# Six stages of a two-layer attention kernel under one block, with a hand-drawn SBUF map and PSUM rings per use

## The reference

```python
# layer 0: cross attention, both sides with an adaptive norm
xq  = (1 + scale_q) * ln(x)   + shift_q        # scale, shift = silu(cond) @ Wss_q + bss_q
xkv = (1 + scale_k) * ln(ctx) + shift_k
x1  = x + softmax(q @ k.T / sqrt(32)) @ v @ Wp + bp
# layer 1
c   = silu(cond) @ W_mod + b_mod               # six vectors of width 512 per batch
qkv = modulate(ln(x1), shift_a, scale_a) @ W_qkv + b_qkv
x2  = x1 + gate_a * (attention(q, k, v) @ W_proj + b_proj)
x3  = x2 + cross_attention(ln(x2) @ W_qc, ln(ctx) @ W_kvc) @ W_cproj + b_cproj
out = x3 + gate_m * (gelu(modulate(ln(x3), shift_m, scale_m) @ W1 + b1) @ W2 + b2)
```

## Time and profile before

| | |
|---|---|
| median of three runs | 2728.22 us |
| profiled execution | 2728.28 us |
| its span (first to last instruction) | 2726.5 us |
| PE busy | 2485.6 us (91%) |
| DVE, ACT, POOL busy | 1393.7 (51%), 1121.4 (41%), 584.0 us (21%) |
| mean granted TensorE clock | 0.94 |

### The profile page before, as it was taken

One profiled execution on the slowest core, in us unless ns is written; L12 is line 12 of the kernel. 1 busy time (PEld: TensorE's weight loads), 2 busy tenths in 40 slices (PEclk: granted clock), 3 DMA queues, 4 the chain that ended last, 5 costly groups with the idle time before them and its releaser, 6 DMA issues. The chain is left out here.

```text
span 2726.5 us, 33092 instructions
## 1 busy us (share of the span) xinstructions
PE 2485.6 (91%) x12304; PEld 1738.5 (64%) x12304; DVE 1393.7 (51%) x2467; ACT 1121.4 (41%) x2007; POOL 584.0 (21%) x321
## 2 busy tenths in 40 slices
PE   5789999879997899999998789999889999999998
PEld 5666666568885344444443366666568888888887
DVE  4346766644444776767676456766534222222221
ACT  5335554334442445555554344444334322332231
POOL 1101111100000356666664501211110000000000
PEclk9878999889998799999998878999889999999999
DMA  7565766545545555544553276767443011101110
GB/s 246 157 189 154 211 189 165 146 153 185 181 178 167 119 123 134 141 122 109 135 125 98 67 195 175 202 180 189 134 129 96 1 54 55 54 1 55 55 39 16
DMA packets 229647, 349.17 MB, mean 128 GB/s; under 512 B 41636, under 2 KB 73468, under 8 KB 229487
## 3 DMA queue, kind: packets, MB, share of 16 engines
q1 hardware_dynamic: 228318, 343.21, 44.2%
q0 software_dynamic: 1168, 3.85, 0.4%
HBM read 228.73 MB, written 116.69 MB: 127 GB/s over the span
## 5 line engine op out<-in xcount | busy, mean ns | idle before, releaser
L1438 DVE TENSOR_REDUCE self_negated_max<-banks 128x1 f32<-128x512 f32 x512 | 334.2, 678 | 161.5 <-PE banks L1505 159.9
L1595 ACT ACTIVATE self_exponentials<-banks 128x512 f32<-128x512 f32 x512 | 287.8, 594 | 305.2 <-PE banks L1526 147.5
L1411 POOL TENSOR_TENSOR self_exponentials<-self_exponentials 128x2048 f32<-128x2048 f32 x64 | 299.7, 4682 | 248.0 <-ACT self_exponentials L1595 248.0
L1956 PE MATMUL banks<-mlp_w_mlp_hi,mlp_hidden_parts 128*128 128x512 f32 x1024 | 334.9, 389 | 1.5 <-DVE mlp_hidden_parts L1914 1.5
L1914 DVE TENSOR_TENSOR mlp_hidden_parts<-mlp_wide,mlp_hidden_parts 128x512 fp32r<-128x512 f32 x128 | 92.9, 726 | 396.9 <-ACT mlp_hidden_parts L1979 396.9
L293 POOL TENSOR_SCALAR norm_rstd<-norm_mean_var 128x4 f32<-128x4 f32 x32 | 8.4, 264 | 1311.4 <-DVE norm_mean_var L265 1311.3
L1505 PE MATMUL banks<-self_key_stack,self_query_stack 96*128 96x512 f32 x512 | 227.6, 456 | 43.4 <-DVE self_negated_max L1438 24.7
L1974 ACT ACTIVATE mlp_wide<-banks,bias_columns 128x512 f32<-128x512 f32 x128 | 88.3, 690 | 425.7 <-PE banks L357 425.7
L1526 PE MATMUL banks<-self_query_stack,self_key_stack 98*128 98x512 f32 x512 | 231.9, 458 | 13.8 <-DVE self_negated_max L1438 9.3
L1956 PEld LDWEIGHTS banks<-mlp_w_mlp_hi,mlp_hidden_parts 128*128 128x128 f32 x1024 | 192.2, 188 | 41.9 <-DVE mlp_hidden_parts L1914 2.0
L1526 PEld LDWEIGHTS banks<-self_query_stack,self_key_stack 98*128 98x128 f32 x512 | 97.9, 192 | 183.3 <-ACT self_exponentials L1595 101.0
(11 more groups left out here) (219 smaller groups left out, 5134.2 us busy)
## 6 DMA issues: line engine op xcount, KB each, us to landing
L_query_stack<-q_parts_L SPq DMA_DIRECT2D x96, 256.0 KB, 4.4
norm_x<-x SPq DMA_DIRECT2D x24, 1024.0 KB, 7.2
self_query_stack<-q_parts_self SPq DMA_DIRECT2D x96, 256.0 KB, 4.1
self_key_stack<-k_parts_self SPq DMA_DIRECT2D x96, 256.0 KB, 6.5
cross_query_stack<-q_parts_cross SPq DMA_DIRECT2D x96, 256.0 KB, 4.5
q_parts_L<-L_query_parts SPq DMA_DIRECT2D x32, 512.0 KB, 4.6
q_parts_self<-qkv_qk_parts SPq DMA_DIRECT2D x32, 512.0 KB, 3.5
k_parts_self<-qkv_qk_parts SPq DMA_DIRECT2D x32, 512.0 KB, 2.8
```

The lines of the kernel that those rows point to most:

```text
L1411: e.tensor_tensor(self.p[kt - 1][:], self.p[kt - 1][:], self.p[kt][:], ALU.add).then_inc(self.paired.sem, 1)
L1438: e.tensor_reduce(self.nm[n % 2][:, h * NT + t:h * NT + t + 1], k.bank[:, self.work.of["max", i], :], AX_X, ALU.max, negate=True).then_inc ...
L1595: e.activation(self.p[kt][:, h, :], k.bank[:, self.work.of["score", i], :], ACT.Exp, scale=SCALE).then_inc(self.exp.sem, 1)
L1956: mm = e.matmul(k.bank[:, self.acc + t, :], l, w, start=j == 0 and q == 0, stop=j == JC - 1 and q == 2)
```

## The change

The six blocks become one. SBUF is no longer allocated by stage: one tensor of the whole size ("arena") is reserved, and each tile is placed in it at a written offset (`alloc_sbuf_tensor_at`). Where a tile lies over one of an earlier stage, its first writer waits for the earlier tile's last reader (`set_freed`). The stages' walks become generators (`run`) that take the next stage's generator as `following` and advance it by some steps in their last groups. The norm scratch, the rows of x, the head tiles, the weight staging and the `wide` tiles are shared by all stages.

- Openings. `Prepare` runs L0's first norm and queries between its context products. L0's last five groups and six steps before its last projection hold Qkv's first norm and first products. Qkv's last batch holds the first self maxima, three steps per product. The last five self groups hold the cross stage's first norm and queries, 12 steps of it before the last projection, and the cross stage's last groups hold the first norm and three first products of the Mlp.
- Modulation. Four of the ten modulation products stay in `Prepare`; six are done beside L0's attention, one per batch from its second on, with two PSUM banks of a ring and one more SBUF tile.
- Queries are made eight groups ahead (were five). The rows of x are asked for inside the first group of a batch (were after it), ahead of the load of values.
- PSUM rings are separate: cross stages have scores (0, 1), maxima and rows (2, 3), products (4, 5), and (6, 7) for value sums, sums, norm transposes and late modulation; the self stage has scores (0, 1), maxima and rows (2, 3, 4), products (5), value sums 6, sums 7; the Mlp's second product lags its first by three steps (was two).
- Splitting. For queries, self keys and queries, context keys and the unmodulated norm, ACT writes only the high part, and DVE computes the low part straight from PSUM with `scalar_tensor_tensor`. The modulated norm keeps its wide tile, from which both parts are made.
- Self values are loaded per group, 256 KB a time (were 1 MB per batch).

```diff
-        prepare.following, l0.following, attention.following, cross.following = l0, qkv, cross, mlp
-        for stage in (prepare, l0, qkv, attention, cross, mlp):
-            with ExitStack() as placed:
-                stage.place(placed)
-                with nc.Block() as blk:
-                    blk.tensor(stage.tensor)
...
+        self.fence = ctx.enter_context(nc.sbuf_tensor("arena", [P, ARENA // 4], F32))
...
+    def at(self, name, shape, offset, dt=F32):
+        return self.nc.alloc_sbuf_tensor_at(name, shape, dt, offset=self.base + offset)
...
+    def run(self, s):
+        mlp = self.mlp.run(s.mlp)
+        cross = self.cross.run(s.cross, mlp)
+        attention = self.attention.run(s.attention, cross)
+        qkv = self.qkv.run(s.qkv, attention)
+        l0 = self.l0.run(s.l0, qkv, self.prepare.late(s.prepare))
+        for stage in (self.prepare.run(s.prepare, l0), l0, qkv, attention, cross, mlp):
+            weave(stage)
...
@@ CrossAttention
-        self.work, self.products, self.heads, self.sums = Turns(range(4)), Turns((4, 5)), 6, 7
+        self.products, self.first_products = k.ring(4, 5), k.ring(*first_banks)
+        self.scores, self.max_banks, self.pairs = k.ring(0, 1), k.ring(2, 3), k.ring(6, 7)
...
+            if g == 0 and b > 0:
+                side.append(after(1, base(b - 1)))
+            if g == 0 and b > 0 and beside:
+                side.append(after(1, some(3, beside)))
-            m = n + self.QUERY
+            m = n + self.lead
...
-            if n >= last - G:
-                side.append(some(3, beginning))
-            weave(attend(n), asking, asking if m % G == G - 1 else None,
-                  after(2, maxima(n + self.MAX)) if n + self.MAX < last else None,
-                  after(2, max_rows(n + self.ROWS)) if n + self.ROWS < last else None,
+            if n >= LAST - G - 1:
+                side.append(some((1, 4, 4, 4, 1)[n - LAST], following))
+            yield from braid(s.attend(n), asking, asking if g >= 2 else None,
+                             s.maxima(n + self.MAX) if n + self.MAX < LAST else None,
+                             s.max_rows(n + self.ROWS) if n + self.ROWS < LAST else None,
...
-            if g == 0 and b > 0:
-                load_base(b - 1)
-        values(last - 1)
-        load_base(B - 1)
-        weave(finish(last - 1))
-        add_base(B - 1)
-        weave(project(B - 1))
+        s.values(LAST - 1)
+        s.load_base(B - 1)
+        yield from s.finish(LAST - 1)
+        yield from some(self.tail, following)
+        s.add_base(B - 1)
+        yield from s.project(B - 1)
...
 # its queries, on ACT and DVE
-            e.activation(self.wides[w][:], src, ACT.Identity, bias=bias, scale=1.0).then_inc(self.q_wide.sem, 1)
-            e.tensor_tensor(self.q_out[n % 2][:, 1, :], self.wides[self.norm.wide_turns.of["query", n]][:], raw(self.q_out[n % 2][:, 0, :]),
-                            ALU.subtract).then_inc(self.q_lo.sem, 1)
+            e.scalar_tensor_tensor(out[:, 1, :], k.bank[:, self.query_ring(n).of["query", n], :], k.bias_cols[:, col:col + 1],
+                                   raw(out[:, 0, :]), ALU.add, ALU.subtract).then_inc(self.q_lo.sem, 1)
...
@@ SelfAttention
-        self.work, self.products, self.heads, self.sums = Turns(range(4)), Turns((4, 5)), 6, 7
+        self.scores, self.max_banks, self.products = k.ring(0, 1), k.ring(2, 3, 4), k.ring(5)
+        self.heads, self.sums = k.ring(6), k.ring(7)
...
+            if n >= LAST - G - 1:
+                side.append(some((1, 9, 4, 10, 10)[n - LAST], following))
```

1918 lines of the change are left out of this document (1063 added, 855 removed).

## The result

| | before | after |
|---|---|---|
| median of four runs | 2729.06 us | 2689.16 us |
| lowest and highest | 2726.59, 2741.58 | 2685.52, 2690.80 |
| ratio, 95% interval | | 0.985 (0.982 to 0.988) |
| span of the profiled execution | 2726.5 | 2688.9 |
| PE busy | 2485.6 | 2475.8 |

The account below looks back on a forecast made before the run. PE was taken as full in the Mlp, so gains had to come from waits and low clock elsewhere. Gross 111.6 + 59.4 + 31.5 + 30 = 232.5, less 32, left 200.5 off 2728.3: 2528 us, range 2455 to 2640.

Parts of the forecast that it names:

- (a): At the stage borders: PE's waits go because neighbouring stages' work fills them, 111.6 us.
- (b): At the five border windows: the low clock's cost goes if PE stays busy through the border, 59.4 us.
- rival 1: Stage borders: openings fill but their waits stay, as the filler arrives late; 124.5 us won, 2604 us; chance 0.26.
- (f): Losses that come back: 12 us at the first self keys, 6 of clock at L0's start, 14 of friction.
- (c): Residual additions: PE's waits, put down to the late load of x, go with an earlier load; 31.5 us.
- (d): Self-attention PSUM rings: third maxima bank and separate score banks gain 30 us, bounds -10 to 59.
- (e): High and low parts: ACT loses one operation per split, DVE reads PSUM instead of SBUF; counted 0.
- Rival 3: Self-attention: the single product bank makes PE wait for gating and POOL's addition; slower, 2844 us; chance 0.05.
- rival 4: No change: self-attention takes back what openings and rings give, 6 us per group; 2728 us; chance 0.03.
- rival 2: More than counted: rings give their full 59 us and the 14 and 6 don't come back; 2479 us; chance 0.06.
- the prediction's formula: Clock cost in a window: 2(1-c)W us at half speed, all idle time taken from it, half the rest lost.

Follow-up runs that it names:

- experiment 12: Changed kernel with the layer-0 context modulated by one ACT operation per chunk instead of eight; ratio 0.984 to the kernel before.
- Experiment 11: Changed kernel without L0's opening inside the preparation, its query weights loaded after the context's; ratio 0.991 to the kernel before, 17 us slower than the change.
- experiment 10: Changed kernel without the cross stage's opening in the last self groups; ratio 0.993 to the kernel before, 22 us slower than the change.
- experiments 1 and 2: Kernel before with only the early load of x, ratio 1.003; kernel before with three product banks and three for the rest in both cross stages, ratio 1.0095.
- experiment 9: Kernel before with only the change's self-stage PSUM rings (scores two banks, maxima and rows three, products one); ratio 0.997, span 10.5 us shorter.

## Why the prediction was wrong

**Openings (a) and clock (b).** The mechanism was right, the size not. The prediction took every wait next to a border as gone. Idle time in the border windows fell from 128 to 70 us and the clock's cost from 59 to 36, but in the whole kernel only by 27.8 us of idle time. One border came out as forecast (L0 to Qkv to self, 42.3 for 44); its filler is Qkv's products, which need no stage's round trip (PE is busy for all of 620 to 800 us). At the last border, cross to Mlp, half came, 14.7 for 28: a wait of 4.4 us for a bank stays. At the other two the filler is the start of an attention stage, which has waits of its own, as rival 1 said. At the start it stands on ACT behind the context's modulations (experiment 12), and nearly all of PE's 13.1 us of waits for normed rows are there; before, these were 3.0 us in the whole kernel. Experiment 11 gives the opening 17 us, but without it the first score comes 24.5 us later than in the kernel before, in part because the first norm is then not computed beside the preparation either. What the start would be with all ten modulations left in the preparation, where they lay between the context products, no run shows; the prediction called the late ones the same work in another place. At the self to cross border filling is worth 22 us (experiment 10), and waits for the gated rows (4.0 at most), for POOL's pair (3.5) and for exponentials stay in it. The step that failed: waits were subtracted, and those of the work put in their place weren't asked for.

**Late keys (f).** 9 us were left for the first self keys, 7.9 measured.

**Rows of x (c).** This is where the reading was wrong. "Which wait for the late load of x" rested on the name of the tile that DVE writes. The tile's own waits (14.2 us in 3 for POOL) say that DVE came late, not x, and experiments 1 and 2 show it: the early load alone left 33.8 us of these waits, a third product bank none. Much of DVE's lateness, some 22 us, lies in operations that are longer than usual beside POOL's bias additions. In the changed kernel the waits fell to 8.1 us all the same, and others took their place in the same batches.

**The cross stages' own rings and order.** The prediction priced rings only for self-attention. In the cross stages three edits move against the batch: maxima asked for two rounds sooner, two rings of two in place of one of four, and a lead of eight. Of the 9 us that two steady cross batches are longer, 2.3 are idle time and the rest a clock that stays low longer (see the last section). Undoing the first two brings steady cross batches from 52.5 to 47.5 us and 0.011 of the time; the third brings 0.006 more, in L0, with overlapping intervals. The growth of L0 and cross by 14 and 29 us, and the 31.5 us of (c) that did not come, are 75 of the missing 160 us, and no rival named it. A sum of waits that are to go has no place for this: the waits that two smaller rings and an earlier request bring were put at nothing. The range ended at 2640, 49 us below the measured 2689.

**Self rings (d).** Right in sign, and in that the third bank gains and the single product bank costs nothing. The size is 2.4 us per steady batch, and 8 us by the ratio of experiment 9 (0.997; 10.5 by its span), where 30 was taken. The upper end of 59 counted PE's 24.7 us for the reduction as won; in their place came 24.4 us for the two score banks. The prediction named this loss and set a bound for it, but took half of the upper end.

**Splitting (e).** ACT's busy time fell from 1121 to 1028 us, and no wait of PE shows it. A low part straight from PSUM takes 678 ns on average where the two-operand subtraction is used, and 750 in the three-operand form:

```profile
L326 DVE TENSOR_TENSOR x_lo<-wide,x_hi 128x512 fp32r<-128x512 f32 x80 | 55.3, 692 | 90.3 <-ACT x_hi L376 89.4
L1153 DVE SCALAR_TENSOR_TENSOR out_parts<-banks,bias_columns,out_parts 128x512 fp32r<-128x512 f32 x64 | 48.0, 750 | 128.9 <-ACT out_parts L1321 128.9
...
L326 DVE TENSOR_TENSOR x_lo<-banks,x_hi 128x512 fp32r<-128x512 f32 x32 | 21.7, 678 | 18.4 <-ACT x_hi L378 18.2
```

The medians are 693, 751 and 691 ns: the form costs about 60 ns, the source nothing. The estimate from the Trainium skill (VectorE: DVE Perf Modes, The TRN2 errata), 65 ns more from PSUM, isn't borne out: with PSUM as the source the same form is 14 ns shorter on average and 2 by the median.

**Rivals.** Rival 3, rival 4 and rival 2 had no part in it. Rival 1 was the right kind, and at 2604 still 85 us too low, since it kept (c) and knew nothing of the cross rings. Three slips of the text on record: the distance of 400 us between the storing and reading of x1 had no row (it doesn't enter the sum), the steady batch of self-attention was derived as 77 us from a window, where the scores give 77.4; and the traces have 1058 DMA issues on SP before and 1112 after, not 569 and 684.

## What to carry to other kernels

Ask of a wait not only which tile ends it but what the engine that writes the tile was doing and waiting for; if it wasn't waiting for the input you want to bring earlier, bringing it earlier need not win anything. Here a wait once per batch had a second one right behind it: try such edits in pairs too, and look at the batch's length, not at the wait that left. Before dividing a PSUM ring, count the banks that each use needs at its peak; one ring of four beat two of two in self-attention, and in the cross stages once the maxima came later. A third bank for products won only where the ring that gave it could spare one. And look at how long an engine's operations last beside another's, not only at their order.

## What the runs showed of the hardware

DVE's operations with SBUF operands alone took longer while POOL's additions ran: in the kernel before, the low part of the heads at 1721.47 lasted 1.36 us, the residual addition from PSUM next to it 0.68, both beside POOL's L1007. The median of the former over the stage is 0.69. The Trainium skill (GPSIMD Engine Reference, 1. Specifications) names interfaces to SBUF that the two engines share, with contention for DVE instructions that have two SBUF inputs or run in a 2-port perf mode; the rows of the heads agree. The normed row at 1719.66, with one SBUF tensor as input, took 1.50 us as well, where its line's median is 0.54, so two tensor inputs are not needed for it; whether it ran in such a mode no row tells.

The clock stayed low after one wait for stretches of different length. One such stretch of the kernel before, behind the wait of 3.0 us that ended at 1723.49, and one of the changed kernel, behind that of 3.5 us that ended at 1723.36:

```profile
1723.60:1727.00 3.40, 3.40 (x10) 1.84 (x14) 0.00 (x0) 0.00 (x0) 0.36 (x1) 0.50 0.85 193
1723.80:1734.00 10.20, 10.20 (x38) 5.96 (x38) 4.15 (x9) 2.49 (x5) 4.97 (x4) 0.50 0.91 271
```

PE is busy all through both, at half the clock. The other waits of the steady cross batches are alike: behind waits of 2.3 to 4.1 us the stretch at half clock is the short one in the kernel before, and behind waits of 2.0 to 3.8 us it is three to four times as long in the changed one. What makes the difference no run shows. The two steady windows have one wait of 2 to 3.5 us per batch each, and a mean clock of 0.96 and 0.90. By the prediction's formula that is 1 us against 6.6 us in two batches. The formula puts all idle time into the stretches at half clock, and these rows have none in them: each window holds two such stretches, full of work, so half of 6.8 us is lost before and half of 20.4 after, 3.4 against 10.2. With the idle time (5.5 against 7.8) that is 9.1 us, the 9 us by which the two batches are longer: three quarters of the growth is the clock.
